# GpSimd in place of ScalarE makes the scaled copies of the turned dt·x, and TensorE turns the first block's input ahead of the unit's side work

## The reference

```
x1  = x @ W_cond(cond).T + b                  # base weight plus 8 conditioned low-rank terms
two directions (forward, flipped), each: xz = x1 @ in_proj.T; xc = silu(conv4(xz[:512]))
  dt = softplus(...), B, C from xc @ x_proj.T;  h[t] = exp(dt*A)*h[t-1] + (dt*xc)*B[t]
  y = sum_n h*C + xc*D;  out += (y * silu(z)) @ out_proj.T       # 512 channels, 16 states n
x2  = x + out;  r = x2 @ W_cond2.T + bias;  a mixture of 8 experts (top 2 of each token) on r
result = x2 + r + the experts' outputs
```

## Time and profile before

| | us |
|---|---|
| runs before | 1413.41, 1414.28, 1415.38; median 1414.28 |
| the profiled execution: own time, span | 1411.67, 1409.9 |
| busy over the span: PE, DVE, ACT, POOL | 1242.3, 900.4, 778.5, 918.0 |
| mean granted TensorE clock, as a share of the full one | 0.937 |

### The profile page before, as it was taken

One profiled execution on the slowest core, in us unless ns is written; L12 is line 12 of the kernel. 1 busy time (PEld: TensorE's weight loads), 2 busy tenths in 40 slices (PEclk: granted clock), 3 DMA queues, 4 the chain that ended last, 5 costly groups with the idle time before them and its releaser, 6 DMA issues. The chain is left out here.

```text
span 1409.9 us, 20902 instructions
## 1 busy us (share of the span) xinstructions
PE 1242.3 (88%) x7120; PEld 942.3 (67%) x7120; DVE 900.4 (64%) x1065; ACT 778.5 (55%) x1477; POOL 918.0 (65%) x511
## 2 busy tenths in 40 slices
PE   8978888888797878788876779999999999999997
PEld 4545564555555555555565654557999999999996
DVE  3988898889889989889898789964111111111110
ACT  4687877688788597697788585523111111111111
POOL 1998998889989889889899887932222222222211
PEclk9989989899999998989899889999999999999998
DMA  5666555555556455555565554516989889988982
GB/s 195 211 179 180 167 176 164 154 183 182 167 171 195 155 175 173 176 172 163 174 198 179 178 163 154 181 46 216 386 315 326 304 320 316 326 305 322 319 314 45
DMA packets 109979, 296.95 MB, mean 211 GB/s; under 512 B 10017, under 2 KB 21922, under 8 KB 94386
## 3 DMA queue, kind: packets, MB, share of 16 engines
q1 hardware_dynamic: 100226, 277.53, 57.3%
q0 software_dynamic: 9648, 18.09, 6.3%
HBM read 277.76 MB, written 9.96 MB: 204 GB/s over the span
## 5 line engine op out<-in xcount | busy, mean ns | idle before, releaser
L1376 POOL TENSOR_TENSOR arena<-arena 128x1024 f32<-128x1024 f32 x192 | 455.1, 2388 | 79.6 <-DVE arena L1096 63.4
L472 PE MATMUL ps_y<-ident,arena 128*128 128x128 f32 x1840 | 263.5, 292 | 58.2 <-POOL arena L1376 57.7
L472 PEld LDWEIGHTS ps_y<-ident,arena 128*128 128x128 f32 x1840 | 228.0, 152 | 107.6 <-POOL arena L1376 79.5
L1428 POOL DMA_INDIRECT out_x<-arena x39 | 61.8, 1585 | 304.9 <-ACT arena L1024 263.3
L871 ACT ACTIVATE ps_de<-arena,An 128x512 f32<-128x512 f32 x196 | 134.9, 688 | 158.3 <-DVE arena L1083 151.1
L871 ACT ACTIVATE arena<-arena,An 128x512 f32<-128x512 f32 x316 | 218.5, 710 | 0.1
L1310 DVE TENSOR_TENSOR arena<-ps_du,arena 128x512 f32<-128x512 f32 x39 | 27.0, 692 | 227.8 <-PE ps_du L720 227.8
L1360 POOL TENSOR_TENSOR arena<-arena 128x1024 f32<-128x1024 f32 x67 | 159.3, 2378 | 3.5 <-DMA arena<-bc_scratch 3.2
L720 PE MATMUL ps_y<-arena 128*128 128x128 f32 x1248 | 153.8, 277 | 0.5 <-ACT arena L1012 0.5
L720 PEld LDWEIGHTS ps_y<-arena 128*128 128x128 f32 x1248 | 149.9, 194 | 2.7 <-ACT arena L1012 0.7
L1068 DVE TENSOR_TENSOR ps_u<-ps_du,arena 128x512 f32<-128x512 f32 x196 | 136.7, 697 | 21.0 <-DVE arena L1108 10.3
(11 more groups left out here) (238 smaller groups left out, 2017.8 us busy)
## 6 DMA issues: line engine op xcount, KB each, us to landing
arena<-bc_scratch SPq DMA_DIRECT2D x256, 512.0 KB, 4.7
arena<-in_W SPq DMA_DIRECT2D x117, 1024.0 KB
arena<-arena POOLq DMA_DIRECT2D x15, 512.0 KB, 5.6
arena<-in_cd SPq DMA_DIRECT2D x16, 256.0 KB, 5.4
out_x<-arena SPq DMA_DIRECT2D x17, 128.0 KB, 5.1
arena<-in_xT SPq DMA_DIRECT2D x2, 1024.0 KB, 6.5
arena<-in_w2c SPq DMA_DIRECT2D x1, 2048.0 KB, 8.7
diag<-in_dd SPq DMA_DIRECT2D x16, 128.0 KB, 5.0
```

The costliest lines, as they stand in the source:

```text
L472: t = e.matmul(Y[j][:, part], src[:, part], ident[:, :], start=False, stop=stop, is_transpose=True, skip_group_check=True)
L1376: e.tensor_tensor(hc[:, i % NP, :, :], hh[:, i % NH, :, :], c, ALU.mult).then_inc(gp_hc, 1)
L1428: e.indirect_dma_start(out, bass.IndirectOffsetOnAxis(dest[:, i:i + 1], 0), yo[:, i % 3, :], None, compute_op=ALU.add).then_inc(l_add, 16)
```

## The change

GpSimd gets the four scaled copies of each flipped unit, as `tensor_scalar` multiplications, placed three units ahead: before product(i) it makes uT of unit i+3. ScalarE's `u_turned` is gone. The semaphore `ac_uT` becomes `gp_uT`. GpSimd waits before them for `ac_kept` (that `duT` and `bT` have been written) and for the previous `first_u`. ScalarE's writing of `duT` and `bT` gets waits on `gp_uT`, since their readers are now on another engine. In TensorE's loop `first_u(i)` moves ahead of `side_work(i)` and so also ahead of `second_u(i+1)`.

```diff
             def second_u(i):
-                e.wait_ge(ac_uT, flips(i))
+                e.wait_ge(gp_uT, flips(i))
...
+                if i < NU and flipped(i):
+                    first_u(i)
                 if i < NU:
                     side_work(i)
                 if i + 1 < NU and flipped(i + 1):
                     second_u(i + 1)
-                if i < NU and flipped(i):
-                    first_u(i)
...
                     e.wait_ge(pe_dT, 2 * (g - 1) + j + 1)
+                    if g > 1:
+                        e.wait_ge(gp_uT, NF * (g - 1))
...
                     e.wait_ge(pe_bT, 2 * qr + h + 1)
+                    if qr >= 2:
+                        e.wait_ge(gp_uT, NF * (4 * qr - 7 + 2 * h))
...
-                for k in range(4):
-                    t = e.activation(uT[:, k, :], duT[:, k, :], ACT.Copy, scale=bT[:, q % 2, th, k, f:f + 1])
-                t.then_inc(ac_uT, 1)
...
-                if i + 1 < NU and flipped(i + 1):
-                    u_turned(i + 1)
...
+            def u_turned(i):
+                q, th, pr, n = unit(i)
+                g = i // 16
+                e.wait_ge(ac_kept, sum(k in t for t in (DU_AT, ROWS_AT) for k in range(16 * g + FLIP)))
+                if flips(i) > 1:
+                    e.wait_ge(pe_u0, flips(i) - 1)
+                f = (n - FLIP) // STRIDE
+                for k in range(4):
+                    t = e.tensor_scalar(uT[:, k, :], duT[:, k, :], bT[:, q % 2, th, k, f:f + 1], None, ALU.mult)
+                t.then_inc(gp_uT, 1)
...
                     step_widths(*STEP_AT[i - 5])
+                if i + 3 < NU and flipped(i + 3):
+                    u_turned(i + 3)
                 product(i)
```

More of the change, by code:

```diff
@@ L254, in build @@
         ac_yT, pe_back = sem("yT"), sem("back")
-        pe_dT, pe_bT, ac_uT, pe_u1, pe_u0, ac_kept = (sem(n) for n in ("dT", "bT", "uT", "pu1", "pu0", "kept"))
+        pe_dT, pe_bT, gp_uT, pe_u1, pe_u0, ac_kept = (sem(n) for n in ("dT", "bT", "guT", "pu1", "pu0", "kept"))
         ac_z = sem("z")
```

## The result

| | before | with the change |
|---|---|---|
| median, us (runs, span of them) | 1414.62 (4: 1413.41 to 1415.38) | 1540.43 (4: 1539.89 to 1545.91) |
| ratio to before, 95% interval | | 1.0899 (1.0873 to 1.0925) |
| span of the profiled execution | 1409.9 | 1538.4 |
| stage from the first du of a flipped group to the last product | 847.56 | 976.50 |

I take the stage here to the end of the very last product, which is one of a single block (L1372, it starts at 933.39 and takes 1.28); the prediction had ended it one instruction earlier, at 933. In the kernel before this stretch is

What follows compares the result with a forecast made beforehand. GpSimd and VectorE, each with work for nearly 90% of the stage, bound it; afterwards GpSimd does. Its work 757.5 + copies 108 + idle 15 = 880.5 us, +35 against 845.9, so 1449 us; range 1418 to 1488.

Steps and rivals of the forecast that it cites:

- The price of a copy: One scaled copy of 128x256 on GpSimd: 0.45 us, 108 us for all 240; likely span 0.31 to 0.62 us.
- The bound from above: Upper limit for a copy on GpSimd: the two-input multiplication of the same 128x256, 0.69 us each, 166 us for 240.
- Rival B: Copies on GpSimd as dear as a two-input multiplication: stage 931.5 us, +86, time 1500 us; chance 13%.
- GpSimd becomes the bound: In the scan stage GpSimd's work, 757.5 + 108 us, sets the length and VectorE no longer does: +35 us; chance 60%.
- the prediction's sum: Length of the scan stage: GpSimd's work 757.5, copies 108 and idle time 15 give 880.5 us.
- The idle time, 15 us: GpSimd's idle time left in the stage: 10 us waiting for VectorE's scans, 5 for small waits; 88.4 before.
- The order, "most of 18 us" by itself: first_u ahead of TensorE's side work cuts VectorE's 32.7 us wait by some 18 us, mostly gained in the kernel before.
- a wait for `first_u` under 15 us: Sign expected in the changed kernel: VectorE waits under 15 us for `first_u` on TensorE, against 32.7 before.
- not a term of its own: TensorE's new order adds no separate gain, as it frees VectorE, no longer the bound; already in the 15 us idle.
- The relief of ScalarE, 4 us: Copies leaving ScalarE make decays earlier: half of the 8.5 us VectorE's `second_scan` waits for them, 4 us.
- The new waits, 0: Waits between GpSimd's copies, `second_u`, `first_u` and ScalarE's writes stay hidden: 0, at worst 1 us at each of 15 group starts.
- Rival D: GpSimd waits behind VectorE, VectorE behind second_u, second_u behind GpSimd's copies: 50 us idle instead of 15, +70, 1484 us; 10%.

## Why the prediction was wrong

The term that decides, the price of a copy, was off by a factor of two. Three steps held (GpSimd as the bound, its idle time, the new waits), and two side terms were too small.

**The price of a copy: this failed.** The prediction built it as 0.17 us fixed, 0.26 us for 256 elements at the memset's rate, and 0.02 for the factor, 0.45 us. The copy takes 0.90 us, and 240 of them keep GpSimd busy for 218.6 us instead of 108. What was wrong is the rate: from the 8-column copy (0.27 us) to the 256-column one (0.90) it is 2.5 ns per column, not 1, so the 256 columns cost about 0.63 us and not 0.26. The bound from above failed too. It was the two-input multiplication at 0.69 us, on the reasoning that an instruction that reads less is not dearer. For 1024 columns, from start to start, a scalar multiplication takes 3.04 us (one row), a two-input product 2.31, and a two-input product whose factor is broadcast along each quarter 1.86. So the number of inputs does not order these prices; why the scalar multiplication is the dearest is not shown. No GpSimd row of the kernel before was a scalar multiplication, which should have made me hold the upper end open: at twice the two-input row the sum would have covered what came. Rival B, "as dear as a two-input multiplication", was the nearest, and by the prediction's own mark (four copies in 2.5 us or more; they took 3.60) it is the one that came. Its price, 0.69 us, and its 1500 us were too low as well.

**GpSimd becomes the bound: right.** In the table below each kernel's stage is its GpSimd busy time plus what is left idle. Idle time falls from 42 to 6 us as work grows (the two-input product, 3 us above the half copies, is the one exception), while the stage grows by 158.5 us for 194.8 us more work. All kernels in it have the new order and the copies on GpSimd.

| copies on GpSimd | GpSimd busy in the stage | idle | stage |
|---|---|---|---|
| 8 columns of one | 776.2 | 41.8 | 818.0 |
| one of four | 811.4 | 24.1 | 835.5 |
| two of four | 863.9 | 10.2 | 874.1 |
| one two-input product | 867.2 | 13.2 | 880.4 |
| four (the change) | 970.9 | 5.6 | 976.5 |

With the copies' measured time alone put in, the prediction's sum is 757.5 + 218.6 + 15 = 991.1 us; with the measured idle time too, 981.7. The measured stage is 976.5.

**The idle time, 15 us: right in kind.** It was 10.2 at the assumed price and 5.6 at the true one. The split was off: I had put 10 us on the waits for VectorE's scans and 5 on small ones, and at the assumed price they are about 3 and 7.

**The order, "most of 18 us" by itself: right in direction, too small.** It is worth 28 us in the medians and 20.5 in the profiled stage, since 25 us of the wait went and not 18. The sign that the prediction named for the changed kernel, a wait for `first_u` under 15 us, did not come: it is 69.0 us at the true price and 16.5 at the assumed one. And "not a term of its own" once GpSimd is the bound is shown by the copies alone: 1.0887 against 1.0899.

**The relief of ScalarE, 4 us: too small** in the old order, where it is 15 us with the copies nearly free. I had counted only the waits of VectorE that the profile puts down to ScalarE's decays (8.5 us); with the copies away the wait for `first_u` fell too, from 32.7 to 25.8. The likely path is a wait in the kernel before that I had not looked at, TensorE's for ScalarE's copies in front of `second_u`, behind which `first_u` stood in the old order:

```profile
PEld ps_de L617 <- ACT arena L884: 22.5, 13, 3.7
```

That this wait carries the gain is not shown by a run of its own. ScalarE's busy time in the stage fell by 87 us, where 102 were forecast.

**The new waits, 0: right.** Rival D would have kept 40 us and more of GpSimd's idle time; the kernel with half of the copies, at the assumed price, has 10.2. TensorE does wait for the copies, 25.9 us there and 98.2 with all four, but GpSimd is not held up by it: in the changed kernel its only idle times are 4.3 us that the profile puts down to no wait and 1.0 us for a DMA.

## What to carry to other kernels

Moving work to an engine that is busy for 90% of a stage is paid nearly in full beyond its idle time (here 218.6 us of copies on an engine with 88 us idle made the stage 128.9 us longer), so the price per instruction on the new engine decides, and it should be measured with the very form of instruction before it is bounded by a neighbour of another kind: here the "simpler" one cost 1.3 times the neighbour and twice the estimate. A change of two parts is to be taken apart: it holds a part that alone gains 28 us, four transposes ahead of TensorE's side work, and a part that alone loses 125 us, and together they lose 126. The order alone is the version to keep, 1388.85 us, 2.1% faster than before.

## What the runs showed of the hardware

The Trainium skill ("GPSIMD Engine Reference", section "Engine selection") calls one-input elementwise work on GpSimd roughly line-rate. The scalar multiplication here took 0.90 us from start to start for 128x256 and 3.04 us for 128x1024, so the measurement speaks against it for this instruction; it has one input and costs more than the two-input product of the same size (0.69 us in the earlier trace rows, 2.31 us in the earlier trace rows). A two-input product with one factor per partition, repeated along each quarter, came out cheaper than the product with C, 1.86 against 2.31 us for 128x1024, in 60 rows; a single 128x256 row of that kind took 1.01 us, more than the 0.72 of two full inputs, so this is shown for the long form only. And an 8-column scalar multiplication still took 0.27 us, so very short ones are mostly a fixed price.
